# Routing of the last layer in a four-layer Flamingo block: fewer operations, and weight blocks, stores and idle outputs in other places

## What is computed

```
x = x + tanh(g_ffn[1]) * moe(layernorm(x), ...)

def moe(x, rw1, rw2, w1, b1, w2, b2):          # D = 256, hidden I = 1024, E = 8
    logits = gelu(x @ rw1) @ rw2
    probs = softmax(logits, axis=-1)
    wgt, idx = top_k(probs, 2)
    out = zeros_like(x)
    for e in range(E):
        Ye = gelu(x @ w1[e] + b1[e]) @ w2[e] + b2[e]
        Ce = gelu(b1[e]) @ w2[e] + b2[e]       # what a token that did not choose e gets
        for k in range(2):
            mask = idx[..., k] == e
            active = any(mask)
            out += active * wgt[..., k:k+1] * where(mask[..., None], Ye, Ce)
    return out
```

## Time and profile before

| | |
|---|---|
| time, median of 3 runs | 463.55 us (462.35 to 466.19) |
| profiled execution, its own time | 465.41 us |
| its span, first to last instruction | 463.4 us |
| TensorE busy | 330.3 us (71%) |
| VectorE busy | 312.9 us (68%) |
| ScalarE busy | 270.2 us (58%) |
| POOL busy | 172.9 us (37%) |
| DMA traffic | 60.48 MB, 130 GB/s mean |
| mean granted clock of TensorE | 0.874 |

### The profile page before, as it was taken

One profiled execution on the slowest core, in us unless ns is written; L12 is line 12 of the kernel. 1 busy time (PEld: TensorE's weight loads), 2 busy tenths in 40 slices (PEclk: granted clock), 3 DMA queues, 4 the chain that ended last, 5 costly groups with the idle time before them and its releaser, 6 DMA issues.

```text
span 463.4 us, 8686 instructions
## 1 busy us (share of the span) xinstructions
PE 330.3 (71%) x2694; PEld 223.4 (48%) x2695; DVE 312.9 (68%) x787; ACT 270.2 (58%) x542; POOL 172.9 (37%) x232
## 2 busy tenths in 40 slices
PE   0084979879999077686866532058899999999990
PEld 0062327644567043554533211046577777777760
DVE  3996698494765038678696277856478877888860
ACT  1725564218517677778668747306077777777760
POOL 2051005252434655342536554110045444544431
PEclk9996898998999658699898557559799999999996
DMA  7800003531093333827331531655467777777622
GB/s 270 332 1 2 0 0 136 70 91 47 0 181 115 94 94 92 161 65 102 88 94 47 149 91 45 172 185 225 152 220 233 234 230 245 256 228 252 171 27 23
DMA packets 27202, 60.48 MB, mean 130 GB/s; under 512 B 4209, under 2 KB 17858, under 8 KB 23970
## 3 DMA queue, kind: packets, MB, share of 16 engines
q1 hardware_dynamic: 21202, 52.67, 36.5%
q0 software_dynamic: 4416, 6.13, 8.1%
q10 hardware_dynamic: 1552, 1.27, 1.0%
HBM read 29.00 MB, written 6.85 MB: 77 GB/s over the span
## 4 chain that ended last, share of the span: by engine, by line
DVE 27%; PE 18%; issue 16%; ACT 15%; DMA 12%; POOL 7%; SPq 2%; ACTq 1%; DVEq 0%; POOLq 0%
DMA STG<-in_l_w_dram 6%; ACT arena L1024 4%; PE bank L1515 3%; PE bank L1497 3%; POOL W L630 3%; POOL arena L630 2%; DVE arena L2117 2%; DVE arena L2122 2%; ACT arena L1031 2%; DVE X L1700 2%; ACT STG L797 2%; DVE stats L1578 2%; PE bank L1124 2%; PE bank L1518 2%; DMA W<-k_parts 2%
## 5 line engine op out<-in xcount | busy, mean ns | idle before, releaser
L1515 PE MATMUL bank<-arena 128*128 x184 | 62.4, 385 | 1.0 <-DVE arena L2122 1.0
L1024 ACT ACTIVATE arena<-arena,B1D 128x128 f32<-128x128 f32 x184 | 57.2, 391 | 8.1 <-DVE arena L2117 7.9
L2117 DVE TENSOR_REDUCE arena<-bank 128x256 f32<-128x512 f32 x92 | 57.1, 679 | 0.5 <-PE bank L1500 0.5
L1852 DVE TENSOR_REDUCE MX<-bank 128x2 f32<-128x512 f32 (+1 forms) x48 | 31.2, 685 | 32.2 <-PE bank L1272 32.1
L630 POOL TENSOR_TENSOR W<-STG,W 128x256 f16<-128x256 f32 x64 | 41.3, 681 | 30.3 <-ACT W L804 30.2
L797 ACT ACTIVATE STG<-STG 128x1024 f32<-128x1024 f32 x32 | 33.7, 1052 | 30.2 <-DMA STG<-in_l_w_dram 28.0
L694 POOL DMA_INDIRECT arena<-token_rows,GI x23 | 22.9, 995 | 75.2 <-ACT WS L1018 47.0
L1518 PE MATMUL bank<-arena 128*128 x184 | 50.7, 276 | 0.0
L707 POOL DMA_INDIRECT out_dram<-arena,SI x23 | 37.0, 1608 | 33.0 <-DMA out_dram<-arena,SI 24.3
L630 POOL TENSOR_TENSOR arena<-STG,arena 128x256 f16<-128x256 f32 x56 | 36.3, 681 | 33.3 <-ACT arena L804 33.3
L2122 DVE SCALAR_TENSOR_TENSOR arena<-arena 128x512 f16<-128x512 f32 x46 | 29.8, 689 | 26.2 <-ACT arena L1031 24.1
(11 more groups left out here) (288 smaller groups left out, 739.0 us busy)
## 6 DMA issues: line engine op xcount, KB each, us to landing
STG<-in_l_w_dram SPq DMA_DIRECT2D x32, 512.0 KB, 3.6
arena<-W SPq DMA_DIRECT2D x16, 1024.0 KB
STG<-W SPq DMA_DIRECT2D x7, 1024.0 KB
arena<-in_l_w_dram SPq DMA_DIRECT2D x2, 1280.0 KB, 11.9
k_parts<-W SPq DMA_DIRECT2D x2, 768.0 KB, 5.5
W<-k_parts SPq DMA_DIRECT2D x12, 128.0 KB, 5.9
arena<-k_parts SPq DMA_DIRECT2D x12, 128.0 KB, 6.4
X<-in_x_dram SPq DMA_DIRECT2D x2, 512.0 KB, 5.8
```

Source lines behind the costliest of these rows:

```text
L1024: ins = nc.scalar.activation(x, x, ACT.Gelu, bias=B1D[:, e, c:c + 1], scale=1.0 / (X_SCALE * W_SCALE))
L1515: nc.tensor.matmul(bank[6 + q][:, :], GDL[:, q, 0, c * P:(c + 1) * P], W2[:, e, c].rearrange("p s d -> p (s d)"), start=(c == 0), stop=Fal ...
L2117: v.tensor_reduce(half, o, AX.X, ALU.add).then_inc(s_dadd, 1)
```

## The change

1. **Choices from PSUM.** Maxima and their indices are taken from the logits themselves, in PSUM, and no longer from the normalised probabilities; the copy of the logits, the maximum and the normalising of all eight fall away. One exponential over the eight differences to the maximum and over the gap of the second choice (GAP, 9 numbers for each token) gives both the sum and the two weights, and it is only needed behind the masks. ScalarE loads the exponential's table ahead with a dummy activation, and takes the gelu of b1 behind the exponential. With that the program has three table loads between the last row copies and the loop (gelu, exponential, gelu); before it was gelu, exponential, and gelu again at the first tile's L1024.
2. **Slots by a scan.** The counts from MSB alone are rounded up to 128 by adding 127 and masking bits; one scan gives where each expert's slots begin and end. AOH is made by sixteen operations of 128 elements that also multiply the token's number in, and TensorE starts on it after each four. BOH is a plain one-hot. Conversions to integers happen in the operation before. The count of each choice (M01B) goes to bank 3 and is used only for COEF.
3. **In the gather's wait.** Half of the idle outputs (64 matmuls) and the transposes of COEF stand ahead of the first tile on TensorE, the other half behind its w1 product. VectorE makes COEF and the low parts of blocks 30 and 31 ahead of the first tile's row copy. POOL clears GB16, between the low parts of blocks 27 and 28, where VectorE did it.
4. **Weights and stores.** Blocks 24 and 25 are split behind the attention's last copy. Block 28 is scaled between the two halves of the router's gelu. SP stores the token rows between loads; DWE is stored by ScalarE behind block 29.

The diff, cut to its core (declarations, and what repeats the words above, are left out):

```diff
+        SPLIT_UNTIL = (12, 12, 12, 8)
...
+            for i in D_BLOCKS[:2]:
+                load_weights(i)
+            store_token_rows(0)
+            for i in D_BLOCKS[2:4]:
+                load_weights(i)
+            store_token_rows(1)
+            for i in D_BLOCKS[4:]:
+                load_weights(i)
...
-            for i in D_BLOCKS[:-2]:
+            for i in D_BLOCKS[:2]:
+                weights_low(i)
+            pool.wait_ge(s_pv, 4 * B)
+            nc.gpsimd.memset(GB16.rearrange("p c e x -> p (c e x)").bitcast(F32), 0.0).then_inc(s_gbz, 1)
+            for i in D_BLOCKS[2:-2]:
...
+                    if steps and SPLIT_FROM[b] <= u < SPLIT_UNTIL[b]:
...
+            for i in C_BLOCKS[B - 1][2:]:
+                weights_split(i)
...
+                (weights_high if h else weights_scale)(D_BLOCKS[2])
+            nc.scalar.activation(WM[:, 0, 0, 0:2], tg[:, 0:2], ACT.Exp).then_inc(s_warm, 1)
+            act.wait_ge(s_dl, 2)
+            act.wait_ge(s_warm, 1)
+            nc.scalar.activation(PR[:, :, :], GAP[:, :, :], ACT.Exp,
+                                 scale=1.0 / (G_SCALE * W_SCALE)).then_inc(s_ex, 1)
             nc.scalar.activation(GB[:, :, :], B1D[:, :, :], ACT.Gelu).then_inc(s_gb, 1)
-            weights_split(D_BLOCKS[2])
-            act.wait_ge(s_dl, 1)
-            nc.scalar.activation(PR[:, :, :], LG[:, :, :], ACT.Exp,
-                                 scale=1.0 / (G_SCALE * W_SCALE)).then_inc(s_ex, 1)
-            for i in D_BLOCKS[3:]:
+            weights_split(D_BLOCKS[3])
+            act.wait_ge(s_dwe, 1)
+            act.dma_start(token_rows[:, D:ROW].rearrange("(t p) e -> p t e", p=P),
+                          DWE[:, :, :].bitcast(U32)).then_inc(s_rows, 16)
+            for i in D_BLOCKS[4:]:
                 weights_split(i)
...
+            for t in range(T):
+                nc.tensor.matmul(bank[5][:, 0:E], ones_b[:, :], MSB[:, t], start=t == 0, stop=t == T - 1)
...
+                mm = nc.tensor.matmul(bank[3][:, 0:2 * E], ones_b[:, :],
...
+                if i % 4 == 0:
+                    pe.wait_ge(s_onehot, 2 + i // 4)
+                mm = nc.tensor.matmul(bank[6][:, T * E:T * E + TILES], AOH[:, i], BOH[:, i],
...
+            idle_outputs(1)
+            transpose_coefficients()
             pe.wait_ge(s_eid, 1)
...
+                    idle_outputs(0)
...
+            logit = bank[6][:, 0:T * E].rearrange("p (t e) -> p t e", e=E)
+            for t in range(T):
+                mark(v.max(DTOP[:, t], logit[:, t]))
+            here()
+            v.tensor_tensor(GAP[:, :, 0:E], logit, DTOP[:, :, 0:1].broadcast_to([P, T, E]),
                             ALU.subtract).then_inc(s_dl, 1)
-            dve.wait_ge(s_ex, 1)
-            step(v.tensor_reduce(LM[:, :], PR[:, :, :], AX.X, ALU.add))
-            step(v.reciprocal(LM[:, :], LM[:, :]))
-            step(v.tensor_tensor(PR[:, :, :], PR[:, :, :], LM[:, :].unsqueeze(2).broadcast_to([P, T, E]), ALU.mult))
+            v.tensor_tensor(GAP[:, :, E], DTOP[:, :, 1], DTOP[:, :, 0], ALU.subtract).then_inc(s_dl, 1)
...
-                mark(v.max(DTOP[:, t], PR[:, t]))
+                mark(v.max_index(DTOPI[:, t], DTOP[:, t], logit[:, t]))
             here()
...
-            step(v.tensor_copy(DTOPF[:, :, :], DTOPI[:, :, 0:2]))
             for k in range(2):
                 mark(v.tensor_tensor(M01[:, :, k], iota_e[:, :].unsqueeze(1).broadcast_to([P, T, E]),
-                                     DTOPF[:, :, k:k + 1].broadcast_to([P, T, E]), ALU.is_equal))
+                                     DTOPI[:, :, k:k + 1].broadcast_to([P, T, E]), ALU.is_equal))
             here()
...
+            v.tensor_copy(M01B[:, :, :, :].rearrange("p t k e -> p (t k e)"),
+                          M01[:, :, :, :].rearrange("p t k e -> p (t k e)")).then_inc(s_m, 1)
+            dve.wait_ge(s_ex, 1)
+            step(v.tensor_reduce(LM[:, :], PR[:, :, 0:E], AX.X, ALU.add))
+            step(v.reciprocal(DTOPF[:, :, 0], LM[:, :]))
+            mark(v.tensor_tensor(DTOPF[:, :, 1], PR[:, :, E], DTOPF[:, :, 0], ALU.mult))
+            step(v.tensor_scalar(RS[:, :], DTOPF[:, :, 0], tg[:, 3:4], 1.0 / (G_SCALE * W_SCALE), ALU.mult, ALU.mult))
+            v.tensor_tensor(DWE[:, :, :], PR[:, :, 0:E], RS[:, :].unsqueeze(2).broadcast_to([P, T, E]),
+                            ALU.mult).then_inc(s_dwe, 1)
...
-            step(v.tensor_copy(NE01[:, :, :].rearrange("p k e -> p (k e)"), bank[5][:, 0:2 * E]))
-            step(v.tensor_tensor(NE[:, :], NE01[:, 0], NE01[:, 1], ALU.add))
-            dve.wait_ge(s_dconst, 8)
-            step(v.tensor_tensor(USED[:, :, :], NE[:, :].unsqueeze(2).broadcast_to([P, E, T]),
-                                 iota_full[:, :].unsqueeze(1).broadcast_to([P, E, T]), ALU.is_gt))
-            step(v.tensor_reduce(NT[:, :], USED[:, :, :], AX.X, ALU.add))
-            step(v.tensor_tensor_scan(ENDT[:, :], ones[:, 0:E], NT[:, :], 0.0, ALU.mult, ALU.add))
-            step(v.tensor_tensor(BASE[:, :], ENDT[:, :], NT[:, :], ALU.subtract))
-            step(v.tensor_scalar(BASE[:, :], BASE[:, :], float(P), None, ALU.mult))
+            step(v.tensor_scalar(NT[:, :], bank[5][:, 0:E], float(P - 1), None, ALU.add))
+            step(v.tensor_scalar(NT[:, :], NT[:, :], 0xFF80, None, ALU.bitwise_and))
+            dve.wait_ge(s_dconst, 7)
+            step(v.tensor_tensor_scan(ENDT[:, 1:E + 1], ones[:, 0:E], NT[:, :], 0.0, ALU.mult, ALU.add))
...
-                                 BASE[:, :].unsqueeze(1).broadcast_to([P, T, E]), ALU.add))
...
+            step(v.tensor_tensor(SLOTM[:, :, :, :], M01[:, :, :, :],
+                                 SLOTQ[:, :, :].unsqueeze(2).broadcast_to([P, T, 2, E]), ALU.mult))
+            with nc.allow_low_precision("slot numbers are below 2 ** 12"):
+                step(v.tensor_reduce(SLOT[:, :, :], SLOTM[:, :, :, :], AX.X, ALU.add))
...
-            v.tensor_tensor(AOH, iota_p[:, :].unsqueeze(1).broadcast_to([P, 2 * T, P]),
-                            flat2(SMODF).unsqueeze(2).broadcast_to([P, 2 * T, P]), ALU.is_equal).then_inc(s_onehot, 1)
-            for k in range(2):
...
+            step(v.tensor_tensor(SDIVF[:, :, :], SLOT[:, :, :], SMOD[:, :, :], ALU.subtract))
+            flat2 = lambda a: a[:, :, :].rearrange("p t k -> p (t k)")
+            v.tensor_tensor(BOH, iota_slot[:, :].unsqueeze(1).broadcast_to([P, 2 * T, TILES]),
+                            flat2(SDIVF).unsqueeze(2).broadcast_to([P, 2 * T, TILES]), ALU.is_equal).then_inc(s_onehot, 1)
+            for i in range(2 * T):
+                ins = v.tensor_scalar(AOH[:, i], iota_p[:, :], SMODF[:, i // 2, i % 2:i % 2 + 1],
+                                      token1[:, i // 2:i // 2 + 1], ALU.is_equal, ALU.mult)
+                if i % 4 == 3:
+                    ins.then_inc(s_onehot, 1)
+
...
+            v.tensor_scalar(EID[:, :], EIDF[:, :], float(E - 1), None, ALU.min).then_inc(s_eid, 1)
...
+            v.tensor_scalar(GI[:, :], slot_token1, -1.0, 0.0, ALU.add, ALU.max).then_inc(s_gi, 1)
...
+            dve.wait_ge(s_gbz, 1)
...
+            dve.wait_ge(s_ne01, 1)
+            step(v.tensor_scalar(ACTV[:, :, :].rearrange("p k e -> p (k e)"), bank[3][:, 0:2 * E], 0.0, None, ALU.is_gt))
+            chosen = DTOPF[:, :, :].unsqueeze(3).broadcast_to([P, T, 2, E])
+            mark(v.tensor_tensor(SLOTM[:, :, :, :], M01[:, :, :, :], chosen, ALU.mult))
+            step(v.tensor_tensor(CF[:, :, :, :], ACTV[:, :, :].unsqueeze(1).broadcast_to([P, T, 2, E]), chosen, ALU.mult))
+            step(v.tensor_tensor(IDLE[:, :, :, :], CF[:, :, :, :], SLOTM[:, :, :, :], ALU.subtract))
+            for r in range(2):
+                mark(v.tensor_tensor(COEF[:, :, r * E:(r + 1) * E], IDLE[:, :, 0], IDLE[:, :, 1], ALU.add))
+            v.tensor_tensor(COEF[:, :, 2 * E:3 * E], CF[:, :, 0], CF[:, :, 1], ALU.add).then_inc(s_coef, 1)
+            here()
```

159 lines of the change are left out of this document (51 added, 108 removed).

## The result

| | before | changed |
|---|---|---|
| time, median of 14 runs each, side by side | 465.11 us (461.96 to 470.12) | 458.33 us (455.57 to 462.12) |
| ratio | | 0.9866, 95% interval 0.9833 to 0.9899 |
| profiled execution, its span | 465.4, 463.4 us | 457.11, 455.4 us |

What follows compares the result with a forecast made beforehand. The chain from the last attention batch through router, slots and gather into the expert loop was taken as the bound. Steps of 2.2 + 3.4 + 0 + 0.8 + 2.7 = 9.1 us off the median 463.55 gave 454.5, range 450.5 to 458.5.

Steps and rivals of the forecast that it cites:

- Step 1: Last attention batch to logits: blocks 24 and 25 leave the attention loop; copy 3.9 us earlier, logits 2.2 gained, bounds 0 and 3.9.
- Step 2: Logits to first use of the ranks: 8.03 us becomes 4.6, 3.4 gained, bounds 1.5 and 3.9.
- the bound of a doubled price: Maxima and indices reading PSUM could cost twice the 1.9 us taken for them, 1.9 more.
- Step 3: Ranks to slots: fewer small operations, but three charged 0.45 us each beside POOL; 0 gained, bounds -1 and +1.3.
- Step 4: One-hot to GI: sixteen AOH operations priced at 2.3 us, no second one-hot; 0.8 gained, bounds 0 and 1.4.
- Step 5: Gather to second tile: gather to first tile unchanged, first to second 12.49 us becomes 9.8; 2.7 gained, bounds 2.0 and 4.7.
- the rival with the early clock: TensorE's clock rises early or VectorE's steps miss POOL: 2 us more gained, 452.5; chance 0.18.
- The one in which step 1 is all given back: Blocks 26 and 27 come still later than reckoned, before the logits: 6.9 us gained, 456.7; chance 0.17.
- wait for the weights' store: The gather waits for the weights' store, or idle outputs hold TensorE: 455.5 to 457 us; chance 0.12.
- The idle outputs did not hold TensorE: Other form of the store rival: idle outputs hold TensorE beyond the rows' landing, 455.5 to 457 us; shared chance 0.12.
- the slower case: Block 31's low half, ahead of the first tile's row copy, comes too late: at 311, 5.7 us slower, 469; chance 0.03.
- The rule weighed: Table loads on ScalarE, three before tile 0: about 2.66 us each by the skill, against 1.28; block 29 then 2.8 later.

Runs made afterwards that it cites:

- Experiment 5: Changed kernel with only the router weights' low parts moved early on VectorE, ahead of the last layer norm: last copy to logits 23.57 us, HV to logits 35.71.
- experiment 6: Changed kernel with both passes of block 28 behind the second half of the router's gelu: HV to logits 37.65 us, last copy to logits 25.51.
- Experiment 1: Kernel before with only blocks 24 and 25 split behind the attention's last copy: 0.9955 of the kernel before, HV to logits 36.02 instead of 37.88 us.
- experiment 8: Changed kernel with block 29 split on ScalarE ahead of the exponential instead of behind the gelu of b1: 462.21 us, logits to GI 12.53.
- Experiments 7: Changed kernel with AOH by four operations of 512 elements instead of sixteen of 128, the token's number multiplied into BOH: 458.86 us, ratio 0.9837.
- experiment 9: Changed kernel with all 128 idle-output matmuls and the coefficients' transposes behind the first tile's w1 product again: 0.9915, first to second tile 10.44 us.
- experiment 10: Changed kernel with the first tile's w2 product between the two halves of the idle shares on TensorE: 0.9648, median 455.83 us.
- experiment 11: Changed kernel with block 27 behind rows 6 and 7, router low parts and half the hidden product early, first tile's w2 product between idle-share halves: 448.62 us, 0.9598.
- 12: The kernel of experiment 11 with AOH by four wide operations and the token's number multiplied into BOH: 447.72 us, 0.9569.

## Why the prediction was right or wrong

The direction and most mechanisms held; the size was too large by about 3 us against the ratio, 1.1 against the profiled pair. The terms missed by more than their sum: steps 1 and 4 brought 1.5 and 1.6 us less than forecast, steps 2, 3 and 5 0.6, 0.5 and 2.1 more, and the stretch behind the second tile lost 1.0. That the sum came so near is in part luck.

**Step 1, forecast 2.2, got 0.7: the term that failed.** The copy came as reckoned (3.9 forecast, 4.12 got), and row 6 stood behind block 27's split. The step that failed is what is given back behind the copy: 1.7 forecast, 3.39 measured. Block 27's split ended 14.6 us behind the copy and not 13.9, since its load was there later, and the last row's low part ended 0.9 later than reckoned. What I left out is that POOL's low half of 27 now runs beside the last small operations on VectorE. The router's low parts took 0.89 and 0.63 us there, 1.0 us more than in the kernel before, and TensorE waited for them. VectorE before, with POOL idle beside it:

```profile
275.57 0.41 DVE L1965 SCALAR_TENSOR_TENSOR arena<-arena 128x256 f16<-128x256 f32 x1
...
275.91 0.15 DVE L1969 SCALAR_TENSOR_TENSOR RW<-RW2R,RW 128x8 f16<-128x8 f32 x1
```

At these prices, an estimate, they would have ended at about 274.5 in the changed kernel, before TensorE's last transposes at 274.75, and nobody would have waited. Experiment 5 shows what the wait is worth: 0.85 to 1.2 us come back when they are moved. The hidden product took 0.57 us more (4.15 against 3.58 us) at a grant of 0.66 against 0.77. And the term I did charge, block 28 between the gelus, was nothing (experiment 6). So of the 1.7 missing 0.9 lies ahead of the low parts' end, and 0.8 behind it: 0.75 of wait and 0.57 of product, less the 0.5 charged for block 28. Experiment 1 puts the step by itself at 1.9, with the same low parts of 0.89 and 0.63; it had 0.7 of that from a faster copy, at a full grant.

**Step 2, forecast 3.4, got 4.0.** Maxima on PSUM cost 0.68 us against 0.65, so the bound of a doubled price is excluded. The exponential was no longer waited for.

**Step 3, forecast 0, got 0.5.** POOL's low half of 29 fell on it (287.28, forecast 285.5), and one cast took 0.59, the one-hot BOH 0.90. I charged 1.3 for such collisions; three operations paid 0.96 together (0.18, 0.42, 0.36), so the charge was right in kind, a little high in size.

**Step 4, forecast 0.8, got -0.8: the second failed term.** I priced sixteen operations of 128 elements at the 2.29 of one operation on 2048, though my own estimate from the small rows said 2.9 and more. They took 4.00, of which 0.35 is POOL's (experiment 8). Experiments 7 and 8 show 0.62 for one operation on 512 elements and 0.91 for four on 128 (3.65 / 4), so the price did not go by the elements. How much of it is the number of operations and how much their form stays open.

**Step 5, forecast 2.7, got 4.8, of which 1.0 went back to the next tile.** The mechanism of the rival with the early clock held in this profile: the grant was 0.50 until 298.5 us, in the 64 idle outputs, and 1.00 through the first tile, and no table load stood at its gelu. In five of eleven profiles it did not (experiment 9), and first to second tile took 9.2 to 9.4, a gain of 3.2, so 1.6 of the 4.8 is luck. And I took the period behind the second tile as untouched. In it the shares wait for VectorE, as they did before the change, the grant falls, and 14.6 to 17.5 us are spent as it happens to rise (experiment 10). The profiled execution of the changed kernel, 457.11 us, was 1.2 below its own median, and that of before 0.3 above; this is the difference between 8.3 and 6.8 us. The lengths of these stretches scatter by more than that from one execution to the next. A sum of one profile's stretches could not be surer than about 2 us here; my range took the early grant in only as a gain.

**The rivals.** The one in which step 1 is all given back came nearest (456.7). Step 1 was given back but for 0.7, in part for its cause: the loads were later than reckoned, but the rest was VectorE beside POOL and the clock. That the total fits too is luck, since the other terms missed as well. The gather did not wait for the weights' store: it stood 0.91 us behind GI, released by VectorE. The idle outputs did not hold TensorE: it still waited 1.20 us for the landed rows, and the first tile was 8.24 behind GI. Block 31's low half ended at 299.4, ahead of the row copy at 301.76, so the slower case was never near.

**The rule weighed.** In the changed kernel the exponential's table load at 281.27 took 1.28 us and the next activation stood at 282.56, so the row's price held. The Trainium skill, page "ScalarE: Activation LUTs", section "What ACT_TABLE_LOAD costs", gives about 2.66 with a drain; no drain shows in this trace either.

## What to carry to other kernels

When an edit moves a chain earlier, look at what runs on POOL at the new time of every small VectorE operation: a step that cost 0.15 us alone cost 0.63 beside it, and TensorE waited. Price many small operations from the small rows of the profile, and not by the rate of a large one: that gave 2.3 us, the small rows 2.9, and it was 3.65 with POOL idle. Where TensorE waits for some 2 us between two pieces of work, look for a ready piece to put between them: here that brought 3.4 us or more, nearly as much as the whole routing rewrite from the logits to GI.

## What the runs showed of the hardware

Beside POOL's 256-element operations a VectorE operation cost up to 0.5 us more, and not by its size: 0.41 to 0.89 on 256 elements, 0.15 to 0.63 on 8, 0.17 to 0.59 for a cast of 16. Others beside the same group of POOL's paid less or nothing: BOH 0.54 to 0.90, SMOD 0.17 to 0.35, and the subtraction SDIVF right behind the cast, at 288.52, took 0.16 (0.17 before, with POOL idle). POOL's four operations took 3.09 us at 272.32, and 2.55 where VectorE left them alone. The Trainium skill, page "SBUF — State Buffer", section "SBUF: two separate sides", says that the two engines share a pair of ports, which one of them holds for a whole instruction. The trace agrees: each rise is less than one of POOL's operations takes alone (2.55 / 4 = 0.64 us).

TensorE's grant stood at either 0.50 or 1.00 wherever a window was short enough to hold one level (1.2 and 2.4 GHz). The same instructions from one tile to the next took 7.7 or 9.3 us, and in the next period 14.6, 15.8 or 17.5, from one run to another, by when it rose. With no wait left in the second period it held at 1.00 in one of three profiles, and the period took 9.50 us (experiment 11). In the other two (10 and 12) it still fell to 0.50 for some 3.5 us, and the period took 11.15. Removing one wait so shortened this stretch and narrowed what executions of it differ by, from 2.9 us to 1.65.
